# Attention inside a three-part block: the values of two neighbouring steps in one run, between the next step's two pairs of scores

## The reference, cut to what matters

```python
x = x + 0.5 * ffn(layernorm(x))                    # weights and activations rounded to 4-bit blocks
q, k, v = (heads(layernorm(x) @ W.T) for W in (Wq, Wk, Wv))   # 16 heads of 16 columns
logits = where(causal, q @ k.T * 16 ** -0.5, -max_float)
attn = softmax(logits)                             # subtracts the row's largest, divides by the sum
x = x + (attn @ v) @ Wo.T
x = x + 0.5 * ffn(layernorm(x))
```

## Time and profile before

| what | value |
|---|---|
| median of 3 runs | 2064.31 us |
| profiled execution, first to last instruction | 2063.7 us |
| attention stage, about 690 to 1554 us | 864 us |
| TensorE busy in it | 852.13 us |
| VectorE busy in it | 771.27 us |
| ScalarE busy in it | 723.57 us |
| GpSimd busy in it | 186.20 us |
| TensorE clock granted in it (1.00 is 2.4 GHz) | 1.00 |

### The profile page before, as it was taken

One profiled execution on the slowest core, in us unless ns is written; L12 is line 12 of the kernel. 1 busy time (PEld: TensorE's weight loads), 2 busy tenths in 40 slices (PEclk: granted clock), 3 DMA queues, 4 the chain that ended last, 5 costly groups with the idle time before them and its releaser, 6 DMA issues. The chain is left out here.

```text
span 2063.7 us, 44136 instructions
## 1 busy us (share of the span) xinstructions
PE 1992.7 (97%) x13211; PEld 1304.7 (63%) x13211; DVE 1872.8 (91%) x4691; ACT 1320.0 (64%) x2267; POOL 1089.4 (53%) x1773
## 2 busy tenths in 40 slices
PE   4999999998998999999999999999999899999999
PEld 3888888887885333333333333333328788888888
DVE  7899999998988899999999999999946899999997
ACT  4455554544774588888888888888894355555453
POOL 6788888885666112222222212222222788888885
PEclk9999999999998799999999999999999999999999
DMA  6000000001676445555545445555326000000000
GB/s 209 19 0 0 0 0 0 0 0 51 240 246 200 91 136 137 138 147 147 141 128 141 139 138 142 135 146 147 111 77 215 6 21 15 21 20 20 15 20 26
DMA packets 134841, 185.02 MB, mean 90 GB/s; under 512 B 24928, under 2 KB 76512, under 8 KB 134368
## 3 DMA queue, kind: packets, MB, share of 16 engines
q1 hardware_dynamic: 132000, 182.11, 30.3%
q10 hardware_dynamic: 2688, 1.05, 0.2%
HBM read 113.90 MB, written 85.98 MB: 97 GB/s over the span
## 5 line engine op out<-in xcount | busy, mean ns | idle before, releaser
L1832 POOL TENSOR_SCALAR_AFFINE_SELECT diag_scores<-diag_scores 128x256 f32<-128x256 f32 (+1 forms) x320 | 148.4, 464 | 695.4 <-ACT diag_scores L1797 687.5
L1334 DVE CUSTOM_DVE_ANT_0 gu_ps<-gu_ps,mask_qk 128x512 f32<-128x512 f32 (+3 forms) x676 | 334.5, 530 | 46.1 <-PE gu_ps L1319 38.0
L1319 PE MATMUL gu_ps<-k_stack,q_stack 96*128 96x512 bf16 (+3 forms) x1031 | 317.6, 340 | 9.6 <-DVE part_max L1334 3.8
L1698 PE MATMUL gu_ps<-probs,v_group 128*17 128x512 f32 (+3 forms) x3072 | 310.0, 491 | 3.0 <-ACT probs L1803 1.8
L928 PE MATMUL gu_ps<-wguT_hi,ffn_xT_hi 128*128 128x512 f32 (+1 forms) x768 | 310.4, 404 | 1.1 <-DVE ffn_xT_lo L697 1.1
L928 PE MATMUL gu_ps<-wguT_hi,ffn_xT_lo 128*128 128x512 f32 (+1 forms) x768 | 289.3, 377 | 0.0
L928 PE MATMUL gu_ps<-wguT_lo,ffn_xT_hi 128*128 128x512 f32 (+1 forms) x768 | 288.8, 376 | 0.0
L912 ACT ACTIVATE ffn_z<-xs,ffn_shift,ffn_rstd 128x256 f32 (+1 forms) x128 | 76.9, 601 | 323.9 <-POOL ffn_shift L779 323.9
L1799 ACT ACTIVATE probs<-hT_ps 128x256 f32<-128x256 f32 (+2 forms) x320 | 259.7, 812 | 11.7 <-PE hT_ps L1674 11.1
L1319 PEld LDWEIGHTS gu_ps<-k_stack,q_stack 96*128 96x128 bf16 x1031 | 94.1, 97 | 272.7 <-DVE part_max L1334 192.6
L1799 ACT ACTIVATE probs<-av_ps 128x256 f32<-128x256 f32 (+2 forms) x320 | 263.2, 822 | 0.6 <-PE av_ps L1679 0.6
(11 more groups left out here) (218 smaller groups left out, 4917.6 us busy)
## 6 DMA issues: line engine op xcount, KB each, us to landing
q_stack<-q_parts SPq DMA_DIRECT2D x192, 128.0 KB, 3.3
k_stack<-k_parts SPq DMA_DIRECT2D x192, 128.0 KB, 3.4
o_all<-o_sb SPq DMA_DIRECT2D x64, 256.0 KB
q_parts<-qkv_parts SPq DMA_DIRECT2D x32, 384.0 KB, 2.7
k_parts<-qkv_parts SPq DMA_DIRECT2D x32, 384.0 KB, 2.7
v_ones<-qkv_vst SPq DMA_DIRECT2D x16, 544.0 KB, 3.9
v_group<-v_ones SPq DMA_DIRECT2D x32, 272.0 KB, 4.2
xs<-in_L_attn_x SPq DMA_DIRECT2D x8, 1024.0 KB, 8.3
```

What stands on the lines that cost most here:

```text
L1319: mm = T.matmul(out[:, e, :], qs[0:STACK, h0 + e, t * P:(t + 1) * P], ks[0:STACK, h0 + e, c * CHUNK:c * CHUNK + w], start=True, stop=True)
L1334: last = V.tensor_tensor_reduce(out=ps[:, e * w:(e + 1) * w], in0=ps[:, e * w:(e + 1) * w], in1=mask_qk[:, CHUNK - w:CHUNK], scale=1.0, sc ...
L1698: mm = T.matmul(o_ps[h * VPAD:h * VPAD + VCOLS, CHUNK - w:CHUNK], vs[:, t, h, :], probs[:, h // 2, i % 2, h % 2, at:at + w], start=first, ...
L1832: G.affine_select(out=block_of, in_=block_of, compare_op=ALU.is_ge, fill=MASKED, base=0, pattern=[[0, 2], [0, count], [1, P]], channel_mul ...
```

## The change

Part 4, the values, is taken out of its place behind the scores and put between part 1 (the end of pair A) and part 2 (the beginning of pair B), and it stands in only six of the ten steps (`VALUES_AT`): step 2 takes the values of steps 0 and 1, step 3 those of step 2, step 5 those of 3 and 4, step 7 those of 5 and 6, step 9 those of 7 and 8, and step 0 of the next group those of step 9. Steps 1, 4, 6 and 8 have none. The units are spread over the new order by a new `SLOTS`; the transposition of the maxima stands at the end of step 5. Values are counted by their own index (`NV` = 10, `FIRST_HALF` = 3), which leaves the counts as they were. The number of copies of the exponentials (`PROBS`) stays 2, and ScalarE's order of work and waits stay the same.

```diff
-            HALF = 3
+            PROBS = 2
+            VALUES = [(i, STEPS[i][0][0]) for i in range(NS)]
+            NV = len(VALUES)
+            FIRST_HALF = sum(j == 0 for _, j in VALUES)
+            VALUES_AT = {2: (0, range(0, 2)), 3: (0, range(2, 3)), 5: (0, range(3, 5)), 7: (0, range(5, 7)), 9: (0, range(7, 9)),
+                         0: (1, range(9, NV))}
+            copied_out = {FIRST_HALF: 3, NV: 0}
...
-            SLOTS = {0: (0, 0, 0, 0, 0), 1: (0, 1, 0, 0, 0), 2: (1, 0, 0, 1, 0), 3: (1, 0, 1, 0, 1), 4: (1, 1, 0, 1, 1),
-                     5: (1, 1, 1, 1, 1)}
+            ORDER = {False: (0, 1, 2, 3), True: (0, 1, 4, 2, 3)}
...
-                for part, count in enumerate(SLOTS[len(left)]):
+                for part, count in zip(ORDER[i in VALUES_AT], SLOTS[i in VALUES_AT, len(left)]):
...
-                                    elif what == "part" and i:
-                                        values(b, g, i - 1)
-                                    elif what == "part" and prev:
-                                        values(*prev, NS - 1)
+                                    elif what == "part":
+                                        back, vs = VALUES_AT[i]
+                                        if not back or prev:
+                                            for v in vs:
+                                                values(*(prev if back else (b, g)), v)
```

More of the change, by code:

```diff
@@ L1442, in attention @@
             NS = len(STEPS)
-            HALF = 3
+            PROBS = 2
[5 more added lines that the diff above has]
+            copied_out = {FIRST_HALF: 3, NV: 0}
+            assert sorted(v for _, vs in VALUES_AT.values() for v in vs) == list(range(NV))
             def columns(j, t):
@@ L1488, in attention @@
                         plan[i].append(("entry", enter(("unit", *left.pop(0)))))
-                    if i == MAX_STEP and part == 4:
-                        plan[i].append(("entry", enter(("turn_max",))))
+                assert not left
+                if i == MAX_STEP:
+                    plan[i].append(("entry", enter(("turn_max",))))
             NE = len(ENTRIES)
@@ L1619, in group @@
                             if nxt:
-                                once(sp, "pv", n * NS, 0)
+                                once(sp, "pv", n * NV, 0)
                                 fill(sp, *nxt)
@@ L1633, in _ @@
                         groups(sp, group)
-                        once(sp, "pv", (NG - GROUPS + 1) * NS, 0)
+                        once(sp, "pv", (NG - GROUPS + 1) * NV, 0)
                         for c in range(A_RING):
@@ L1683, in score_head, with values @@
                                 mm.then_inc(s[pairs[pair][0]], 1)
-                        def values(b, g, i):
+                        def values(b, g, v):
                             vs = ring[g % RING][2]
                             n = b * GROUPS + g
+                            i, half = VALUES[v]
                             for name in ("probsA", "probsB"):
@@ L1692, in values @@
                                 once(pe, "diag", n * len(DIAG), DIAG.index(i) + 1)
-                            first, last = i in (0, HALF), i in (HALF - 1, NS - 1)
+                            first, last = v in (0, FIRST_HALF), v in (FIRST_HALF - 1, NV - 1)
                             if first:
-                                once(pe, "o_sb", n * 2, i // HALF)
+                                once(pe, "o_sb", n * 2, half)
                             for j, t, at, w in pieces(i):
@@ L1743, in _ @@
                         groups(pe, group)
-                        values(*LAST, NS - 1)
+                        for v in VALUES_AT[0][1]:
+                            values(*LAST, v)
                     @block.scalar
@@ L1789, in group @@
                                     load_max(*nxt)
-                                d = DIAG.index(i) if i in DIAG else None
-                                first = 0 if d is None else on_diag[i] * P
+                                to = i % PROBS
                                 for pair, (sc, pr) in enumerate(pairs):
                                     once(act, sc, n * NS, i + 1)
-                                    once(act, "pv", n * NS, i - 1)
+                                    once(act, "pv", n * NV, i - 1)
+                                    first = on_diag[i] * P if i in DIAG else 0
                                     if first:
```

18 lines of the change are left out of this document (10 added, 8 removed).

## The result

| kernel | median | runs | ratio to before, 95% interval |
|---|---|---|---|
| before | 2064.59 us | 2063.94 to 2066.43, 4 | |
| changed | 2198.84 us | 2197.11 to 2199.48, 4 | 1.0646 [1.0631, 1.0661] |

The change costs 134 us. The profiled execution of the changed kernel took 2199.12 us, its span 2197.3.

What follows compares the result with a forecast made beforehand. The prediction saw TensorE as the apparent bound before, no engine far behind; after, TensorE and ScalarE wait in turn. Six stretches sum to 31.71 us a group against 27.25; 4.46 x 32 = 143 us more gives 2207 us, range 2140 to 2250.

Steps and rivals of the forecast that it cites:

- T(i): The moment when pair B of step i has been streamed on TensorE; the prediction sums waits from one to the next.
- T(5) to T(7): From pair B of step 5 through step 6's copies, mask, masked exponential and values to pair B of step 7: 6.77 us.
- T(7) to T(9): From pair B of step 7 through exponential A of step 8 and two steps of values to step 9's pair B: 5.54 us.
- T(9) to T(0): From pair B of step 9 through its exponential and one step of values to pair B of step 0: 3.24 us.
- T(0) to T(2): From step 0's pair B through masked exponential, copy out, step 1's exponential A and two steps of values: 6.41 us.
- T(2) to T(3): From pair B of step 2 through copy, mask, masked exponential and half-step values to pair B of step 3: 3.44 us.
- T(3) to T(5): From step 3's pair B through copy out, step 4's exponential A and two steps of values to step 5's pair B: 6.31 us.
- What the change takes away: Ten runs of values become six on TensorE, saving four pairs of edges: 0.88 us a group.
- Half covered: Rival: half of the 5.3 us of TensorE waits a group goes, giving 29.0 us a group, 2121 us; chance 0.07.
- faster: Rival: saved edges decide and the order does not, 26.37 us a group, 2036 us; chance 0.07.
- Nothing to measure: Rival: edges saved and waits gained cancel at 0.88 us a group, 2060 to 2068 us; chance 0.02.
- The clock falls: Rival: TensorE's waits drop its clock to 1.2 GHz for a fifth of the stage, 2307 us; chance 0.03.

Runs made afterwards that it cites:

- e4: Changed kernel with VectorE's reductions reading only 64 columns of each tile: 2186.85 us, ratio 1.0585.
- e5: Changed kernel with ScalarE's exponentials taken over half their columns, the masked ones kept whole: 2172.61 us, ratio 1.0521.
- e9: Changed kernel with both cuts of e4 and e5, reductions over 64 columns and half exponentials: 2124.19 us, ratio 1.0292.
- e6: Kernel before, with a unit put between the two pieces of values in two steps, so twelve runs a group: 2080.36 us, ratio 1.0080.
- e1: Changed kernel with ten runs of values again, each between the pairs of the next step: 2360.32 us, ratio 1.1418.
- e2: Changed kernel with its six runs of values placed behind both pairs of scores: 2157.31 us, ratio 1.0445.
- e7: Kernel before with eight runs behind pair B (steps 1 and 2, 7 and 8 merged) and a third, half-wide exponentials copy: 2084.25 us, ratio 1.0100.
- e10: e2 with a third, half-wide copy of the exponentials for steps 2 and 8: 2136.65 us, ratio 1.0365.
- e11: Kernel before with nine runs, step 2 taking the values of steps 0 and 1 between its pairs: 2080.03 us, ratio 1.0079.
- e8: The eight runs of e7 behind pair B, with only two copies of the exponentials: 2124.27 us, ratio 1.0295.

## Why the prediction was right

**The sum.** 2207 us were predicted, 2198.84 measured; 31.71 us a group against 31.49, and 0.22 x 32 = 7 us is nearly the whole difference. Each T(i) is the start of the second matmul of pair B plus the time that its columns take (0.22 us, in step 2 0.11), in the group from 1000 us; e4, e5 and e9 are medians over 26 groups. The last column is what half the exponentials should give by the terms of the chain and the prices of e5's expectation.

| stretch | predicted | measured | e4 | e5 | e9 | halved |
|---|---|---|---|---|---|---|
| T(5) to T(7) | 6.77 | 7.04 | 6.90 | 7.05 | 6.51 | -0.63 |
| T(7) to T(9) | 5.54 | 5.16 | 5.16 | 5.13 | 4.74 | -0.52 |
| T(9) to T(0) | 3.24 | 3.23 | 3.23 | 2.83 | 2.83 | -0.42 |
| T(0) to T(2) | 6.41 | 6.31 | 6.30 | 5.88 | 5.88 | -0.75 |
| T(2) to T(3) | 3.44 | 3.43 | 3.43 | 3.43 | 3.43 | 0 |
| T(3) to T(5) | 6.31 | 6.31 | 6.31 | 5.90 | 5.56 | -0.75 |

Four stretches agree within 0.1 us, and e9 shortens the stretches much as the chains say it should, the one without a plain exponential not at all: so the chains over ScalarE set the time. In the other two a term is mis-sized, 0.38 us too large and 0.27 too small; that they nearly cancel in the sum is luck.

- In T(7) to T(9), "two steps of values 1.74" is wrong by the prediction's own: one of the two is step 8, which has half the columns, so it is 0.87 + 0.44 = 1.31, and the stretch would have been 5.11.
- In T(5) to T(7) a unit that waits for the bank of the transposition was put at nothing, though it "can add about 0.2 us". It waits 0.20 us, and ScalarE waits for pair B behind it: the copy of pair B comes 0.78 us after the start of exponential A of step 6 (1018.44) instead of 0.49. A second unit waits 0.30 us ahead of the values, but costs nothing: the values of step 6 wait for the masked exponential, until 1021.73. With VectorE light (e4) this stretch alone gets shorter. The changed kernel:

```profile
1016.48 0.38 PE L1689 MATMUL av_ps<-q_stack,k_stack 98*128 98x512 bf16 x1
...
1018.57 0.40 PE L1319 MATMUL xd_ps<-k_stack,q_stack 96*128 96x128 bf16 x4 [0.20 <-DVE mT L1880]
...
1019.22 0.59 ACT L1815 COPY diag_scores<-av_ps 128x512 f32<-128x512 f32 x1 [0.20 <-PE av_ps L1689]
...
1020.36 0.39 PE L1319 MATMUL xd_ps<-k_stack,q_stack 96*128 96x512 bf16 x1 [0.30 <-DVE part_max L1334]
...
1020.67 1.06 ACT L1821 ACTIVATE probs<-diag_scores 128x1024 f32<-128x1024 f32 x1 [0.36 <-POOL diag_scores L1850]
...
1023.52 0.38 PE L1689 MATMUL av_ps<-q_stack,k_stack 98*128 98x512 bf16 x1
...
1028.68 0.38 PE L1689 MATMUL av_ps<-q_stack,k_stack 98*128 98x512 bf16 x1
```

One name is wrong in the prediction: the values with two runs of four heads (128 and 384 columns) in the earlier trace rows are those of step 6, not 5. No number hangs on it.

**What the change takes away.** 0.88 us of edges a group: there, in six runs without an edge inside, and its price confirmed by e6, 0.23 us for a way in and out. It did not show in the time, since TensorE's own work no longer set the length of a group.

**What it moves.** The waits stand where the prediction put them. TensorE: 0.80 us before pair A of step 2, 0.95 before the values of step 2, 0.45 before pair B of step 8 and 0.51 before pair A of step 5 (0.6 to 1.1 were said; two are shorter). ScalarE before pair B of steps 0, 3, 5 and 7: 1.23, 0.87, 0.61 and 1.05, released by TensorE, where 0.8 to 1.3 were said; one is shorter.

**What the prediction did not separate.** It gave the loss to the place "between" and counted the pairing as gain. By e1 and e2 both parts lose alone: the place 9.20 us a group with ten runs (8.31 at the full clock), the pairing 2.99. Together they lose 4.24. It fits that six runs lay bare fewer hand-overs than ten: 0.6 x 8.31 - 0.88 = 4.1 us is an estimate of that, but no run tests it.

**The rivals.** "Half covered" (2121) and "faster" (2036) fall: 31.49 - 26.37 = 5.1 us of the 5.3 us of waits are met. "Nothing to measure" falls. "The clock falls" did not happen in the groups of the changed kernel, 1.00; it was granted 0.66 in one late stretch, from 1670 to 1680 us, where no units are left, and it fell again and again in the stage of e1. The PSUM Bottleneck rule in the Trainium skill's "TensorEngine Tiling (Array Packing)", taken over busy totals, would have let the gain pass; the totals of after still do (each emptying engine is busy less than the 26.37 us), and the group takes 31.49.

## What to carry to other kernels

When two engines hand work to each other through single buffers, follow the chain of hand-overs in the order as it will be, and compare its length with the busy time; here the longer of the two was the group, 31.5 us against 26.4. Before work is moved or merged, ask what it covered where it stood: here the values covered ScalarE's hand-over and VectorE's reductions at once, 0.99 us of cover given up for an edge of 0.22. When one wait is taken away, look for the next one before its gain is counted: e5, e7, e10 and e11 each found another one behind it. The chain is only as good as its list of waits: it held for the changed kernel and for e1, and the expectations of e2, e7, e8 and e10, which set waits against edges too, missed.

## What the runs showed of the hardware

**The clock in e1.** TensorE waited up to 1.64 us at a time in e1, and the granted clock over its stage (706 to 1798 us) was 0.97. TensorE after one of these waits, then that stretch in busy times (the third number from the end is the clock):

```profile
1036.82 1.91 PE L1713 MATMUL gu_ps<-probs,v_group 128*17 128x128 f32 x16 [1.64 <-ACT probs L1820]
1038.66 0.61 PE L1319 MATMUL gu_ps<-k_stack,q_stack 96*128 96x512 bf16 x1
1039.07 0.63 PE L1688 MATMUL av_ps<-q_stack,k_stack 98*128 98x512 bf16 x1
1039.49 0.63 PE L1319 MATMUL gu_ps<-k_stack,q_stack 96*128 96x512 bf16 x1
```

```profile
1036.80:1039.90 3.10, 3.08 (x19) 1.00 (x20) 0.59 (x1) 0.79 (x1) 0.00 (x0) 0.50 0.00 0
```

512 columns take 0.42 us there instead of 0.22: the level of 1.2 GHz. The lower clock did not come behind every such wait, though each group has one of 1.64 us: of the 30 groups eleven took 35.56 or 35.57 us and one 35.23, all at 1.00, the others 36.56 to 37.82 at 0.91 to 0.95. So a group with a fall took 1.0 to 2.3 us more. The Trainium skill, "TensorE: Matmul & The Clock Gate", section on psum-queue depth-cycling, tells of a kernel whose clock goes back and forth when TensorE idles briefly between groups of matmuls; e1 agrees with that; the groups of the changed kernel with units in them (waits up to 1.0 us in the same view, clock 1.00) do not show it.

**The edge.** The Trainium skill, "TensorEngine Tiling (Array Packing)", section Key Properties, says that a change of tiling mode drains TensorE. The runs price the edge here: 0.10 us into and 0.12 out of a run of values that are tiled by 32 columns, between matmuls over the whole array, and e6's 0.23 us for the pair. That a drain is the whole of it no run shows, since the type changes there too, from bf16 to f32.
